# Four transformer layers in one kernel: when VectorE's small operations run in the attention layers, and how semaphores are cleared

## The reference

```python
# layer 0: adaptive norm, attention with 16 heads of 32, q and k normalized, MLP of 2048 with gelu
qn = q / jnp.maximum(jnp.linalg.norm(q, axis=-1, keepdims=True), 1e-12) * sm
kn = k / jnp.maximum(jnp.linalg.norm(k, axis=-1, keepdims=True), 1e-12)
p = jax.nn.softmax(jnp.einsum('bhqd,bhkd->bhqk', qn, kn) + attn_bias, axis=-1)
x = x + (einsum(p, v) @ Wproj.T + bproj) * gamma1
x = x + (gelu((_ln(x) * (scale2 + 1.0) + shift2) @ Wfc1.T + bfc1) @ Wfc2.T + bfc2) * gamma2
# layer 1: adaptive norm, rotary embedding, sparse window attention, 16 heads of 32; x = x + out
# layer 2: adaptive rms norm, rotary embedding, attention with 8 heads of 64 and one k/v head,
#          then silu(h @ Wg.T) * (h @ Wu.T) @ Wd.T; both added to x
# layer 3: eight experts of 64 -> 256 -> 64 with gelu, adaptive norm, silu, a product with 512x512, added to x
```

## Time and profile before

| | |
|---|---|
| time, median of 3 runs | 2793.87 us (2792.99 to 2800.02) |
| time of the profiled execution | 2805.94 us |
| its span, first to last instruction | 2804.2 us |
| mean granted TensorE clock | 0.908 |
| busy: PE, DVE, ACT, POOL | 86%, 56%, 46%, 32% |

### The profile page before, as it was taken

The page is one execution under the profiler, slowest core; times in us unless marked ns, Lnnn a source line. Parts: engine busy times, 40 slices in busy tenths (PEclk is TensorE's granted clock), DMA queues, the critical chain, the costliest instruction groups (busy, mean ns, idle before and its releaser), DMA issues. The chain is left out here.

```text
span 2804.2 us, 47282 instructions
## 1 busy us (share of the span) xinstructions
PE 2407.7 (86%) x15672; PEld 1952.3 (70%) x15672; DVE 1560.3 (56%) x4470; ACT 1279.6 (46%) x3188; POOL 902.2 (32%) x988
## 2 busy tenths in 40 slices
PE   6888888897699999588788768889899999996776
PEld 4777777786487888466565557777688888885565
DVE  5867767776553434565556466557543333334866
ACT  3666766767321111377665656566531111102443
POOL 0333343423476667123222213223211211211321
PEclk8889999998899999778778679999999999997898
DMA  6000000000110100210000010000100000001000
GB/s 253 1 2 2 9 2 9 2 9 16 61 46 16 44 2 0 74 61 2 2 1 1 1 42 1 1 0 1 46 23 23 23 23 22 0 0 49 8 23 31
DMA packets 17096, 65.29 MB, mean 23 GB/s; under 512 B 3293, under 2 KB 4061, under 8 KB 12277
## 3 DMA queue, kind: packets, MB, share of 16 engines
q1 hardware_dynamic: 16884, 62.70, 6.2%
HBM read 57.42 MB, written 5.28 MB: 22 GB/s over the span
## 5 line engine op out<-in xcount | busy, mean ns | idle before, releaser
L1948 POOL TENSOR_TENSOR l2m_hidl<-l2m_hid,l2m_hidh 128x512 fp32r<-128x512 f32 x64 | 101.0, 1578 | 449.2 <-DVE l2m_hidh L1918 449.2
L1093 ACT ACTIVATE l0a_prob<-l0a_prob,l0a_nmin 128x512 f32<-128x512 f32 x256 | 185.5, 726 | 120.5 <-DVE l0a_nmin L1375 120.0
L1813 ACT ACTIVATE l2m_gate<-l2m_psG 128x512 f32<-128x512 f32 x64 | 38.3, 599 | 437.5 <-PE l2m_psU L1744 436.7
L1570 POOL TENSOR_TENSOR l0a_prob<-l0a_prob,l0a_rinv 128x512 f32<-128x512 f32 x64 | 66.9, 1046 | 483.2 <-DVE l0a_rinv L1382 483.2
L1913 DVE TENSOR_TENSOR l2m_hid<-l2m_gate,l2m_psU 128x512 f32<-128x512 f32 x64 | 44.0, 688 | 282.3 <-ACT l2m_gate L1813 282.3
L1105 ACT ACTIVATE l0a_PT<-l0a_psT 128x512 f32<-128x512 f32 x256 | 152.0, 597 | 55.0 <-PE l0a_psO L946 35.0
L1375 DVE CUSTOM_DVE_ANT_0 l0a_prob<-l0a_psS,l0a_mask 128x512 f32<-128x512 f32 x256 | 175.4, 689 | 1.9 <-PE l0a_psS L904 1.4
L1968 POOL TENSOR_TENSOR res_X<-res_X,l0m_share 128x512 f32<-128x512 f32 x128 | 162.9, 1300 | 24.5 <-DVE l0m_share L1902 23.3
L925 PE MATMUL l0a_psT<-res_ident,l0a_prob 128*128 128x128 f32 x1024 | 165.4, 287 | 3.6 <-ACT l0a_PT L1105 3.3
L780 PE MATMUL l0a_psA<-res_l0a_wh,res_hTh 128*128 128x128 f32 (+1 forms) x512 | 156.0, 305 | 12.7 <-PEq L75 6.7
L1817 ACT ACTIVATE l0m_hid<-l0m_psG,l0m_b1c 128x512 f32<-128x512 f32 x64 | 43.9, 690 | 266.6 <-PE l0m_psG L1744 266.6
(11 more groups left out here) (410 smaller groups left out, 7678.7 us busy)
## 6 DMA issues: line engine op xcount, KB each, us to landing
res_l2m_stage<-in_l2m_w SPq DMA_DIRECT2D x8, 1536.0 KB, 6.5
res_l0m_stage<-in_l0m_w SPq DMA_DIRECT2D x8, 1024.0 KB, 4.8
cond_w<-in_wmod SPq DMA_DIRECT2D x6, 1024.0 KB, 15.8
res_X<-in_x SPq DMA_DIRECT2D x4, 1024.0 KB, 14.2
l1a_wmod<-in_wmod SPq DMA_DIRECT2D x4, 1024.0 KB, 5.8
out<-res_X SPq DMA_DIRECT2D x16, 256.0 KB, 2.0
l_stage<-in_l_w SPq DMA_DIRECT2D x3, 1024.0 KB, 6.9
cond_stage<-in_l0a_w SPq DMA_DIRECT2D x3, 768.0 KB, 13.3
```

The source lines that it names most:

```text
L1093: act.activation(prob[:, n % NP, 0:w], src[:, 0:w], ACT.Exp, bias=nmin[:, n % NP:n % NP + 1], scale=-1.0, accum_out=ssum[:, n % NP:n % NP ...
L1570: op = pool.tensor_tensor(x, x, r.to_broadcast([P, w]), ALU.mult)
L1948: pool.tensor_tensor(hidl[:, s % 2, m, :], hid[:, m, :], f32(hidh[:, s % 2, m, :]), ALU.subtract).then_inc(hl_done, 1)
```

## The change

`close` clears runs of consecutive semaphore numbers with one instruction each. In `attention`, the chain for the inverse root in `prepare` starts at s = 6 for every group, goes on at s = 7 together with `qk_factors`, and `qk_scale` comes at s = 9. The five parts of `inverse_deviations` come 0, 1, 4, 5 and 5 steps after the last tile's statistics. The statistics start at other steps: in the first batch of layer 2 one later, in the last batch two later in layer 0 and three earlier in layer 2, there with a `drain` ahead of each tile. `norm_factors` comes one step later, in the step of the first `norm_rows`.

```diff
+    def runs(self):
+        nums = sorted(s.num for s in self.sems)
+        firsts = [n for n in nums if n - 1 not in nums]
+        return [(n, next(m for m in range(n, nums[-1] + 2) if m not in nums)) for n in firsts]
...
-                for s in self.sems:
-                    sp.sem_clear(s)
+                for first, after in self.runs():
+                    sp.sem_clear(range(first, after))
...
-        FIRST_AT = NT * NT + 1 if is2 else 2
+        FIRST_AT = NT * NT + 2 if is2 else 2
         LAST_TILE = (B - 1) * NT
-        LAST_AT = 12 if is0 else 10 if is1 else 9
+        LAST_AT = 14 if is0 else 10 if is1 else 6
+        SMALL_AT = {0: (0,), 1: (1,), 4: (2,), 5: (3, 4)}
...
                     if 0 <= i < last - first:
+                        if is2:
+                            v.drain()
                         tile_stats(first + i)
-                    else:
-                        inverse_deviations(v, R, i - (last - first), first, last, eps, rms)
+                    for part in SMALL_AT.get(i - (last - first), ()):
+                        inverse_deviations(v, R, part, first, last, eps, rms)
...
-                        if p == 4:
+                        if s == 6:
                             rsqrt_guess(v, *qk_tiles)
                             rsqrt_newton(v, *qk_tiles)
-                        if p == 5:
+                        if s == 7:
                             rsqrt_newton(v, *qk_tiles)
-                        if p == 6:
                             qk_factors(hg)
-                        if p == 7:
+                        if s == 9:
                             qk_scale(hg)
...
-                        if x == -2:
+                        if x == -1:
                             norm_factors(bn)
```

## The result

| | before | after |
|---|---|---|
| median of 6 runs | 2796.99 us (2792.99 to 2802.20) | 2754.26 us (2749.38 to 2761.46) |
| ratio, 95% interval | | 0.9848 (0.9829 to 0.9867) |
| span of the profiled execution | 2804.2 us | 2753.5 us |
| its granted clock | 0.908 | 0.917 |
| busy in the first attention layer: PE, idle rest | 594 of 689 us, 95 | 582 of 660.6 us, 78 |

The change takes 42.7 us; the forecast was 2753 after a sum of 40.7. The two profiled executions differ by more, 50.7 us of span: 28.0 in the first attention layer, 11.4 in the clears, 6.7 in the second attention layer, and 7.1 in the two MLPs and layer 3, where nothing but the clears between them changed. The third attention layer is 2.0 us longer and `condition` 0.5.

A forecast was written before the change was run, and what follows sets the result against it. TensorE leads the first attention layer but idles for VectorE's minima, held behind a chain that collides with GpSimd. 8.3 + 9.3 + 10 + 2 + 11.1 = 40.7 us; 2805.9 - 40.7 - 12.1 gives 2753 us, range 2737 to 2781.

The forecast's parts named there:

- the statistics: All three attention layers: statistics' parts and `norm_factors` at new steps gain 2 us together, between -2 and 5.
- groups 0 and 1: First attention layer: shorter TensorE waits for minima, recovered idle time kept because later steps have enough work; 9.3 us.
- the clock: First attention layer: fewer lower-clock stretches behind TensorE's waits; 10 us, between bounds of 0 and 25.6.
- The clears: Between stages: about 12 range clears in place of 196 single ones, all on the path; 11.1 us.
- Group 2, the chain: First attention layer: minima of steps 5 and 6 pass the chain, `weigh` starts 2.9 us earlier, four times; 11.6 us.
- Group 2, the loss: First attention layer: `norm_split` queued behind `qk_scale` delays TensorE about 1.1 us in three of four batches; 3.3 us lost.
- rival A: The wait changes place to the minimum of step 7 or 8; attention layers give 3 us, 2780; chance 0.18.
- Rival B: Clock no longer falls behind step 4, giving 25.6 us in place of 10; 2738 us; chance 0.12.
- C: Chain costs the same wherever it stands, only the clears' 11.1 us count; 2783 us; chance 0.04.
- D: Slower: new idle time in steps 6 to 8 brings four more long lower-clock stretches, 10.2 us each; chance 0.04.

The follow-up runs named there:

- the first six: Kernel before, twice, and with only the clears, the statistics, `norm_factors` or the small parts changed; means 175.3 us in group 2, 320.0 in groups 0 and 1.
- the four executions: Changed kernel twice, changed kernel with `LAST_AT` 10, and kernel before with only `prepare` moved; mean 314.6 us in groups 0 and 1.
- the filler: Kernel before, with one step's scores product in group 2 made 13 times to fill TensorE's wait, nothing moved; 2795.17 us, ratio 0.9996.
- The two halves of it that were run: Kernel before with only `norm_factors` one step later, 2799.32 us; kernel before with only `SMALL_AT` (steps of the five parts of `inverse_deviations`), 2798.53 us.
- `prepare` alone: Kernel before with only the chain and the scaling of q and k moved in the first attention layer; 2778.53 us, ratio 0.9907.

## Why the prediction was right, point by point

The forecast was 2753 us and the measured time 2754.3. Most of the mechanism was right, but the closeness is in part luck, because errors cancelled. Group 2 was priced 2.8 us too low, the statistics 2 to 4 too low, groups 0 and 1 about 4 too high and the clock 4 to 7 too high. The time that it started from was also 3.1 us below the later median of six (2793.87 for 2796.99), and its sum 2.0 below the measured gain.

**The clears** were right: 11.1 forecast, 11.4 in the trace and 1.6 behind it, 14 (9 to 18) in the timing. There are 9, not about 12.

**Group 2, the chain** was right in its mechanism and its price. The minima of steps 5 and 6 came ahead, the chain was expected at 2.2 us and took 2.30, and `weigh` starts 3.05 us earlier against the minimum of step 4 (3.27 for 6.32), where 2.9 was forecast. Over all 16 chains of the layer the second instruction, 1016 ns in the median before, now has a median of 181. The run with the chain at step 5 shows that two minima ahead are needed and one is not enough, and the run with the chain ahead of the reciprocals shows that the collision cost time by itself. An undisturbed group 2 goes from 42.5 to 39.7 us, 2.8, and 42.5 to 39.8 in batch 3: 11.1 for four, where 8.3 was forecast.

**Group 2, the loss** was the step that failed in detail: "about 1.1 us lost, in three of four batches", for `norm_split` queued behind `qk_scale`. `qk_scale` takes 1.52 us, but `norm_split` still waits 1.29 us for TensorE, so it is not late. What is late is the minimum of step 7, rival A's place; through the exponential and ScalarE's copy of V it gives TensorE the wait of 1.45 us. Against that the later wait for ScalarE's copy of q and k falls from 2.2 to 0.6. The waits of TensorE in that group, changed kernel:

```profile
PE l0a_psA L836 <- ACT l0a_qT L1097: 2.4, 3, 1.7
PE l0a_psA L790 <- ACT l0a_V L1079: 1.4, 1, 1.4
PE l0a_psS L914 <- DVE l0a_nmin L1387: 1.3, 2, 1.1
PE l0a_psA L836 <- ACT l0a_xn L997: 0.9, 1, 0.9
PE l0a_psA L790 <- ACT l0a_raw L1012: 0.6, 1, 0.6
PE l0a_psO L956 <- ACT l0a_PT L1115: 0.5, 1, 0.5
```

and the kernel before (second execution, batch 2, its 42.49 us group):

```profile
PE l0a_psS L904 <- DVE l0a_nmin L1375: 4.6, 3, 3.3
PE l0a_psA L780 <- ACT l0a_raw L1002: 2.2, 1, 2.2
PE l0a_psA L826 <- ACT l0a_qT L1087: 1.6, 3, 0.8
PE l0a_psA L826 <- ACT l0a_xn L987: 0.9, 1, 0.9
PE l0a_psO L946 <- ACT l0a_PT L1105: 0.4, 1, 0.4
```

9.7 us of idle time became 7.1 by these rows, and TensorE's busy time went from 32.77 to 32.29. 2.6 and 0.5 make 3.1, the 2.8 within 0.3. Of the 3.3 us that the minimum gives back, about 1.4 is spent again on ScalarE.

**Groups 0 and 1** had the right sign and too much: 9.3 forecast, 5.4 by the groups, and 9 as the difference of two timings (26 less 17) that are each good to about 5. The waits of 4.14 and 1.78 us became 0.79 and none, but their groups are only 0.8 us shorter each, 1.1 and 0.6 in the means of the first six and of the four executions. What failed is "the recovered idle time is kept". In the stretch of group 0 of batch 0 TensorE now does 12 more products (240 for 228) and has 32.27 us of work in place of 29.27; so it is 3.0 us of work further on when the group ends, and the group is hardly shorter for it. What sets the end of these groups was not followed up. Only group 1 of batch 0, with its wait of 2.56 us, is 3.1 us shorter, and 4.6 to 5.0 against the other five of the first six executions (37.8 to 38.2 for 33.3). Of group 0 of batches 2 and 3, with 1.0 each in the forecast, batch 2 gives nothing and batch 3 0.9 in the mean, with 1.2 between executions of one kernel. The run with the chain ahead of the reciprocals has 310.8 us in groups 0 and 1, 3.8 less than the move, so in these groups the later place of the parts gives some of the gain away again.

**The clock** was over-sized. Its term was 10 of 25.6 us, with 1.7 for each short stretch and 10.2 for each long one. By the filler a short one costs nothing at that place, and a long one costs 5.8 to 6.5. The long ones stood in 4 of 24 groups 2, 0.67 in an execution, which makes about 4 us on average. The 16.7 us of group 2 less the 11.1 of the undisturbed ones is 5.6, but part of that belongs to the statistics in batch 3. By the two executions with the move and the old statistics (161.0 and 161.3) it is 14.1 less 11.1, 3 us. So the term was 3 to 6 us. The first profile happened to hold two long stretches, and the prediction took them as the kernel's. It was saved by its choice below the middle and by the 2.8 us of an undisturbed group 2, where the forecast's 8.3 makes 2.1 each. Rival B (the clock does not fall any more, 2738) is false: the filler kept it higher (0.95 over the layer for 0.92 and 0.93) and gave no time, and in the changed kernel a short stretch now stands behind the 1.45 us wait. From its stretches view:

```profile
315.10:318.50 3.40, 3.40 (x17) 3.04 (x16) 2.69 (x8) 2.65 (x7) 0.30 (x1) 0.50 0.00 0
```

**The statistics** were under-sized: 2 us forecast, between -2 and 5. By the groups of the second attention layer groups 1 and 2 of batch 0 give 2.6, in all but one execution, and group 1 of batch 3 gives 1.0; in the first layer groups 1 and 2 of batch 3 together go from 78.4 and 79.2 (the two kernels with only `prepare` moved) to between 76.5 and 76.9 in the three with the statistics, about 2; the third layer gives at most 1.9 in its last batch, loses 1.6 there (2.1 was forecast) and gives nothing in its first, where 1.9 was expected. That is 4 to 6. The drains, 1 us in the forecast, were not run alone. "Hidden behind ScalarE and TensorE or give some tenths" is the sentence that failed. The timing of this part, 13 us (8 to 17), stands above it. The two halves of it that were run give 2 and 4.

**Rivals.** C, only the clears count (2783), is false: `prepare` alone gives 26 us, and the chain at step 5 in place of 6 costs 9 to 11. The rule of the Trainium skill (VectorE: DVE Perf Modes, Rules for kernel authors) asks for few operations in a chain and does not speak of their place. Read as if the number were all, it does not hold here: the number is the same, and the rows of the three places show 3.24, 2.91 and 2.30 us and a wait of TensorE of 3.30, 0.92 and none for the next minimum needed. A had its place right and its size wrong: the late minimum of step 7 costs TensorE 1.45 us of 3.3, not nearly all. D did not come in the changed kernel: it has no stretch of 20.5 us at the lower clock in groups 0 to 2. But it can happen: the run with the chain at step 5 has one, in group 0 of batch 0, and that group takes 41.4 us where the changed kernel's takes 38.0.

**Open.** The three parts alone, timed, multiply to 0.9951 x 0.9907 x 0.9954 = 0.9813, 52 us, where the whole gives 0.9848. Each has an interval of about 5 us either way, so the difference of 10 us may be chance; that parts share a gain (the clock of an execution above all) is not excluded. Which half of the statistics part carries what in the second layer is not settled. One version was not tried: the chain ahead of the reciprocals in groups 0 and 1, where that run's 310.8 us is the lowest sum of all, and at step 6 in group 2.

## What to carry to other kernels

A chain of small dependent operations on one engine should stand behind the work that the other engines need next, as many items of it as they run ahead. Moving it by one step too few gave back 10 of 42 us. Ask of every recovered wait who is late next: of 3.3 us a copy of ScalarE took 1.4 back, and in group 0 of batches 0 and 1 waits of 4.14 and 1.78 us gave about 1 us and 0.6. Profile the kernel before twice when the clock is part of the sum, since one execution's low-clock stretches are a sample.

## What the runs showed of the hardware

- VectorE's small operations are slower in GpSimd's time. With the chain wholly inside it (at step 5) four of its five instructions take about 0.60 us in place of 0.17 to 0.19; beside GpSimd's instruction with two tensors one took 1.01. GpSimd's scaling instruction (L1583) has a mean of 838 ns after the change and 758 before. It may meet more of VectorE's work now, which was not tested alone; TensorE's waits for it in this layer are 0.3 us at most. The minimum of 128x512 at 303.28, in the middle of GpSimd's burst, takes its usual 0.69 us.
- The long stretches of 20.5 us at the lower clock come after 3.0 to 3.2 us of waiting, but not in every batch nor in every execution: after the same wait there is mostly a stretch of 3.4 or 6.8. Without that wait they did not occur in group 2 in eight executions, the filler's among them.
- A stretch of 3.4 us at the lower clock can be free, where it only makes TensorE late for something that is late itself (42.5 us for the group with it and without).
- At the barrier ahead of the second MLP 3.5 us of idle TensorE brought 3.4 us or more at the lower clock in eight of nine executions, and 1.5 us brought none in five.
- A clear of a range (up to 45 numbers, split over 9 clears in all) takes 32 to 100 ns by the profile; 45 single ones took 3.0 us.
